# Attention scan in chunks of 64 tokens instead of 128, in a one-core audio tower kernel

## The reference

```python
def step(carry, inp):
    A, z = carry
    qt, kt, vt = inp
    A = lam[None, :, :, None] * A + kt[..., None] * vt[..., None, :]
    z = lam[None] * z + kt
    St = jnp.einsum('bhi,bhij->bhj', qt, A)
    Zt = jnp.einsum('bhi,bhi->bh', qt, z)
    return ((A, z), (St, Zt))
_, (S, Zs) = jax.lax.scan(step, (A0, z0), (qT, kT, vT))
...
att = (S / Zs[..., None]).reshape(Bx, Tx, Cx)
att = g * att @ Wo.T
x = x + att
h2 = layernorm(x, ln2_g, ln2_b)
x = x + jax.nn.gelu(h2 @ W1.T, approximate=False) @ W2.T
```

## Time and profile before

| | us |
|---|---|
| median of 3 runs | 1092.09 |
| span of the profiled execution | 1090.0 |
| TensorE (PE) busy | 1058.7 (97%) |
| VectorE (DVE) busy | 886.6 (81%) |
| ScalarE (ACT) busy | 702.5 (64%) |
| GpSimd (POOL) busy | 293.5 (27%) |

### The profile page before, as it was taken

The page is one execution under the profiler, slowest core; times in us unless marked ns, Lnnn a source line. Parts: engine busy times, 40 slices in busy tenths (PEclk is TensorE's granted clock), DMA queues, the critical chain, the costliest instruction groups (busy, mean ns, idle before and its releaser), DMA issues.

```text
span 1090.0 us, 44778 instructions
## 1 busy us (share of the span) xinstructions
PE 1058.7 (97%) x18851; PEld 800.2 (73%) x18851; DVE 886.6 (81%) x2749; ACT 702.5 (64%) x1258; POOL 293.5 (27%) x177
## 2 busy tenths in 40 slices
PE   6789999999999999999999999999999999999987
PEld 6668677877767778687877867777786777868664
DVE  6889788888988879788887988878788887979642
ACT  3357676576666757576575767657676675758643
POOL 5322132331223222132332223232122322213120
PEclk9799999999999999999999999999999999999999
DMA  5532133122312322132232312313242232214110
GB/s 179 168 91 88 52 94 102 60 89 72 125 51 74 106 76 89 51 127 70 65 97 73 108 51 78 117 59 89 60 130 57 74 105 77 71 51 127 52 39 18
DMA packets 51510, 91.55 MB, mean 84 GB/s; under 512 B 9552, under 2 KB 26608, under 8 KB 51312
## 3 DMA queue, kind: packets, MB, share of 16 engines
q1 hardware_dynamic: 51312, 88.69, 26.7%
HBM read 19.50 MB, written 9.78 MB: 27 GB/s over the span
## 4 chain that ended last, share of the span: by engine, by line
PE 95%; DVE 2%; ACT 1%; issue 1%; POOL 0%; DMA 0%; SPq 0%; DVEq 0%; ACTq 0%; POOLq 0%
PE bank L999 13%; PE bank L1004 11%; PE bank L1148 11%; PE bank L1170 10%; PE bank L1141 10%; PE bank L1176 10%; PE bank L1103 7%; PE bank L1078 4%; PE bank L1081 3%; PE bank L1121 3%; PE bank L1164 3%; PE bank L1086 3%; PE bank L1125 3%; PE bank L1041 3%; PE bank L1030 2%; PE bank L1056 1%
## 5 line engine op out<-in xcount | busy, mean ns | idle before, releaser
L1170 PE MATMUL bank<-xa,f1w 128*128 128x512 f32 (+1 forms) x256 | 120.5, 575 | 0.9 <-issue 0.9
L1148 PE MATMUL bank<-w,hid 128*128 128x128 f32 x1024 | 119.7, 275 | 1.5 <-ACT hid L565 1.5
L1141 PE MATMUL bank<-c,w 128*128 128x512 f32 (+1 forms) x256 | 119.2, 570 | 0.9 <-ACT c L559 0.9
L1148 PEld LDWEIGHTS bank<-w,hid 128*128 128x128 f32 x1024 | 116.9, 192 | 2.9 <-ACT hid L565 2.9
L539 ACT ACTIVATE px<-bank 128x512 f32<-128x512 f32 (+1 forms) x128 | 72.8, 568 | 63.5 <-PE bank L1086 55.2
L419 POOL TENSOR_TENSOR rr<-vv,nhalf 128x4 f32<-128x4 f32 x32 | 32.4, 1012 | 294.9 <-DVE vv L823 294.9
L565 ACT ACTIVATE hid<-bank 128x512 f32<-128x512 f32 (+1 forms) x128 | 70.2, 565 | 63.7 <-PE bank L1141 61.9
L1176 PE MATMUL bank<-hid,f2w 128*128 128x512 f32 (+1 forms) x256 | 107.5, 563 | 0.0
L1103 PE MATMUL bank<-qx,ki 128*32 128x16 f32 x7680 | 102.2, 193 | 1.5 <-DVE ki L866 1.5
L1103 PEld LDWEIGHTS bank<-qx,ki 128*32 128x32 f32 x7680 | 92.7, 110 | 13.7 <-issue 13.7
L804 DVE COPY_PREDICATED px<-mask,bank 128x512 f32<-128x512 uint32 (+1 forms) x128 | 88.5, 691 | 13.5 <-ACT px L539 13.5
(11 more groups left out here) (142 smaller groups left out, 2447.9 us busy)
## 6 DMA issues: line engine op xcount, KB each, us to landing
qx<-qq SPq DMA_DIRECT2D x256, 96.0 KB, 2.2
hs<-hs SPq DMA_DIRECT2D x32, 532.0 KB, 3.9
v<-v_f SPq DMA_DIRECT2D x16, 512.0 KB, 6.0
gz<-gate_f SPq DMA_DIRECT2D x16, 512.0 KB, 3.0
xT<-in_xT SPq DMA_DIRECT2D x16, 468.5 KB, 3.2
f1w<-in_fc1T SPq DMA_DIRECT2D x16, 256.0 KB, 3.2
f2w<-g_dram SPq DMA_DIRECT2D x16, 256.0 KB, 3.3
out<-t_sum SPq DMA_DIRECT2D x16, 256.0 KB, 2.5
```

Source lines behind the costliest of these rows:

```text
L1141: mm(dst[:, 0:width[g]], w1[:, P * j:P * j + P], c1[:, cols(g)], start=True, stop=True).then_inc(w1_ok, 1)
L1148: last = mm(dst[:, P * i:P * i + P], hid[:, j, P * m:P * m + P], w2[:, j, :], start=(j == 0), stop=(j == 3))
L1170: mm(dst[:, 0:width[g]], f1w[:, P * j:P * j + P], xa[:, cols(g)], start=True, stop=True).then_inc(f1_ok, 1)
```

## The change

The scan's chunk is 64 tokens. The level `kw[1]` falls away, with its products (line 1078), its copies of keys and queries, and a sixth of each `qx` transfer. Scores become compact: 64 queries wide instead of 128. Both kinds of scores of a tile, between and inside groups, share one bank, and two banks (5 and 6) take turns; `pairs_a` and `pairs_b` are one function `pairs`, whose end releases ScalarE's copy. The products inside groups have 64 keys as weights and 4 x 8 queries as columns: 16 a full tile. The scan has 14 states; `us`, `chain` and `states` work on twice as many, and `scan` does 64 columns at a time. For the states of the two halves of a tile, `v` becomes two tiles, each with the other half of its partitions zero, filled by two DMAs; `us` reads them too and so waits for the DMAs, and `hand_v` stands in SyncE's order ahead of `spread(b, 0)` of the same sample. In `scan`, tile 0 now waits for the states.

```diff
 SyncE
-                sp.dma_start(v[:, :, :], v_f[:, :, :]).then_inc(v_in, 16)
+                for o in (0, 1):
+                    rows = slice(BLK * o, BLK * o + BLK)
+                    sp.dma_start(v[o][rows, :, :], v_f[rows, :, :]).then_inc(v_in, 16)
...
-                    hand_h2(b); hand_v(b); spread(b, 1); hand_gate(b); spread(b, 2); spread(b, 3)
+                    hand_h2(b); spread(b, 1); hand_gate(b); spread(b, 2); spread(b, 3)
...
-                    hand_h1(b); spread(b, 0)
+                    hand_h1(b); hand_v(b); spread(b, 0)
 ScalarE, pxs
-                n = WIN * windows[c]
-                act.wait_ge(pa_ok, nth(b, TILES, c + 1))
+                n = BLK * blocks[c]
+                act.wait_ge(pr_ok, nth(b, TILES, c + 1))
 VectorE, qlev, between
-                for at, m, skip in ((Q8, EIGHT, 0), (Q32, 2 * WIN, WIN), (Q64, P, P // 2)):
+                for at, m, skip in ((Q8, EIGHT, 0), (Q32, 2 * WIN, WIN)):
...
-                klevels(b, g, parts + [(kw[:, 0, :], 2 * WIN, WIN, WIN), (kw[:, 1, :], P, P // 2, P // 2)], kon_ok)
+                klevels(b, g, parts + [(kw[:, :], 2 * WIN, WIN, WIN)], kon_ok)
 TensorE, us
-                pe.wait_ge(v_ok, nth(b, 2, 2))
-                for c in range(NST):
+                pe.wait_ge(v_in, nth(b, 32, 32))
+                for i in range(NST):
                     for hd in range(HEADS):
                         r = slice(HD * hd, HD * hd + HD)
-                        last = mm(dst[r, c:HD * NST:NST], kcT[:, c, r], v_f[:, c, r], start=True, stop=True)
+                        last = mm(dst[r, i:HD * NST:NST], kcT[:, i // 2, r], v[i % 2][:, i // 2, r], start=True, stop=True)
 TensorE, pairs
-                if c:
-                    pe.wait_ge(px_ok, nth(b, TILES, c))
+                if c >= 2:
+                    pe.wait_ge(px_ok, nth(b, TILES, c - 1))
                 else:
-                    before(pe, px_ok, b, TILES, TILES)
+                    before(pe, px_ok, b, TILES, TILES - 1 + c)
...
-                if n == NW:
-                    t0 = Q64 + P // 2 * o
-                    for w in (0, 1):
-                        r = slice(WIN * w, WIN * w + WIN)
-                        mm(O[r, :, P // 2:P], kw[:, 1, k0 + WIN * w:k0 + WIN * w + WIN], x[:, :, t0:t0 + P // 2], start=True, stop=True)
...
                 for j in range(EIGHT):
-                    for w in range(n):
-                        t0 = P * (c % 2) + WIN * w
-                        last = mm(D[WIN * w:WIN * w + WIN, :, WIN * w + j:WIN * w + WIN:EIGHT], ki[:, j, k0 + WIN * w:k0 + WIN * w + WIN],
-                                  x[:, :, t0 + j:t0 + WIN:EIGHT], start=True, stop=True)
-                last.then_inc(pb_ok, 1)
+                    for o in range(blocks[c]):
+                        r, s0, t0 = slice(BLK * o, BLK * o + BLK), k0 + BLK * o, q0 + BLK * o
+                        last = mm(D[r, :, j:BLK:EIGHT], ki[:, j, s0:s0 + BLK], x[:, :, t0 + j:t0 + BLK:EIGHT], start=True, stop=True)
+                last.then_inc(pr_ok, 1)
 TensorE, scan
+                opened = False
+                for o in range(blocks[c]):
+                    i, t = 2 * c + o, s0 + BLK * o
+                    if i:
+                        for hd in range(HEADS):
+                            r = slice(HD * hd, HD * hd + HD)
+                            mm(S[r, t:t + BLK], ab[:, i - 1, r], qc[:, BLK * i:BLK * i + BLK], start=not opened, stop=False, skip_group_check=True)
+                        opened = True
+                pe.wait_ge(px_ok, nth(b, TILES, c + 1))
+                for o in range(blocks[c]):
+                    t = s0 + BLK * o
                     for hd in range(HEADS):
                         r = slice(HD * hd, HD * hd + HD)
-                        mm(S[r, s0:s0 + n], ab[:, c - 1, r], qc[:, P * c:P * c + n], start=True, stop=False, skip_group_check=True)
...
+                        last = mm(S[r, t:t + BLK], v[o][:, c, r], px[c % 2][:, hd, :], start=False, stop=True, skip_group_check=True)
```

More of the change, by code:

```diff
@@ L65, in program @@
     windows = [min(4, WINS - 4 * c) for c in range(TILES)]
-    NST = TILES - 1
+    blocks = [-(-windows[c] // 2) for c in range(TILES)]
+    NBLK = sum(blocks)
+    NST = NBLK - 1
+    KT = TILES - 1
     ctx = ExitStack()
@@ L91, in program @@
         zeros = sb("zeros", P)
[L92 removed]
+        tick = sb("tick", 5)
         nhalf = sb("nhalf", 2 * TILES)
@@ L207, in program @@
         place = {name: (i, n) for i, users in enumerate(USES) for n, (name, _) in enumerate(users)}
-        spare = [bank[i] for i in range(8) if i not in [BETWEEN, DIAG] + [place[n][0] for n in ("dct0", "dct1", "nT0", "nT1")]]
+        spare = [bank[i] for i in range(8) if i not in [*PAIRS] + [place[n][0] for n in ("dct0", "dct1", "nT0", "nT1")]]
         EARLY = 5
@@ L665, in _ @@
             V.memset(dec[:, :, :], 0.0).then_inc(s_pw, 1)
-            V.memset(bank[DIAG][:, :], 0.0)
-            V.memset(bank[BETWEEN][:, :], 0.0)
+            for i in PAIRS:
+                V.memset(bank[i][:, :], 0.0)
+            for tile in px:
+                V.memset(tile[:, :, :], 0.0)
+            V.memset(v[0][BLK:P, :, :], 0.0)
+            V.memset(v[1][0:BLK, :, :], 0.0)
             for tile in (k, ga, gate_f, c1, xa):
@@ new lines, in pairs @@
+                    pe.wait_ge(kin_ok, nth(b, 2, c // 4 + 1))
+                for o in range(blocks[c]):
+                    r, t0 = slice(BLK * o, BLK * o + WIN), Q32 + q0 // 2 + WIN * o
+                    mm(O[r, :, WIN:BLK], kw[:, k0 + BLK * o:k0 + BLK * o + WIN], x[:, :, t0:t0 + WIN], start=True, stop=True)
+                for j in range(1, NE):
+                    for w in range(windows[c]):
+                        r, t, s0 = slice(WIN * w, WIN * w + WIN), WIN * (w % 2) + EIGHT * j, k0 + WIN * w
+                        t0 = Q8 + q0 + WIN * w + EIGHT * j
+                        mm(O[r, :, t:t + EIGHT], ko[:, j - 1, s0:s0 + WIN], x[:, :, t0:t0 + EIGHT], start=True, stop=True)
```

134 lines of the change are left out of this document (56 added, 78 removed).

## The result

| | before | after |
|---|---|---|
| median of 4 runs each, us | 1092.66 | 1171.43 |
| ratio, 95% interval | | 1.0717 (1.0677 to 1.0757) |
| span of the profiled execution, us | 1090.0 | 1168.4 |

The change makes the kernel 79 us slower. The direction was forecast, the size was not: 36 us were forecast, and 1171 lies above the range that ended at 1150. Four executions in this document took 1513 to 3488 us where all others took 1083 to 1175; they are left out of every time and ratio, and g1, whose profiled execution is one of them, has no profile to read.

What follows compares the result with a forecast made beforehand. TensorE was taken as the bound, busy all 64.74 us of a round. Terms +2.5 - 2.9 + 0.9 + 0.6 + 1.0 = +2.1 us a round, times 16, plus 2 at the start, gave 1128 us, 8-in-10 range 1068 to 1150.

Steps and rivals of the forecast that it cites:

- Part 1: Inside products: 16 steps of 57 ns at 64-wide weights, +0.30 us a full tile, +2.5 us a round.
- Part 3: Changes of weight width on TensorE: nine more a round at 0.10 us each, +0.9 us a round.
- Part 2: Products between halves: one level goes, -0.41 us in each of 7 tiles, -2.9 us a round.
- The line between 32 and 128 wide: Inside products: step interpolated from 33 ns at 32-wide and 107 ns at 128-wide weights, giving 57 ns at 64.
- Part 4: Twice the states: `us` +0.5 and `scan` +0.1 us a round, GpSimd's spreading of about 5.1 us hidden.
- Part 5: Values ahead of queries: TensorE waits before tile 0's first product, +1.0 us a round, plus 2 us once at the start.
- signs that the forecast named: Tile 3's inside group about 1.0 us, `us` about 0.95, round near 66.8, about a microsecond's wait before tile 0.
- two signs of being wrong: Tile 3's inside group at or under 0.6 us, or no wait before tile 0.
- the weights' width is not the price: Rival: 64-wide inside products step like 32-wide ones, 33 ns; most of it near 1078 us; chance 0.20.
- the two without late queries: Rivals with no query wait before tile 0: 1110 us (0.15), or 1095 us with no drain at width changes either (0.08).
- loads and columns in turn: Rival: inside products' columns don't stream beside the next weight load, 84 ns a step, 1181 us; chance 0.05.

Runs made afterwards that it cites:

- g1: e3 with the two value tiles in one, so the states take 28 products (56 records) instead of 56 (112): 1084.97 us, ratio 0.9921.
- g2: g1 with the states' products also moved ahead of the second half of the weights products, apart from tile 1: 1085.71 us, ratio 0.9925.
- g6: g2 with the 64-wide inside products of the changed kernel: 1135.77 us, ratio 1.04.
- e1: The changed kernel with the query transfers issued ahead of the value transfers again: 1151.25 us, ratio 1.0533.
- e4: The kernel before with only the inside products made wide (64 keys as weights, 4 x 8 queries as columns): 1155.66 us, ratio 1.0564.
- h3: e4 with queries read and results written in runs of 8 instead of every eighth place: ratio 1.0515.
- g4: The kernel before with inside products still 32 keys wide but 4 x 8 queries as columns instead of 4 x 4: 1138.25 us, ratio 1.0413.
- k1: g4 with queries read in runs of 8, results still written to every eighth column: ratio 1.0.
- e3: The changed kernel with queries first again and inside products 32 keys wide again: 1116.72 us, ratio 1.0208.
- g3: The kernel before with the states' products issued twice, 112 records instead of 56: 1109.57 us, ratio 1.0147.
- h2: e4 with results written in runs of 8, queries still read at every eighth place: ratio 1.0584.
- h1: e4 with queries read in runs of 8, results still written to every eighth column: ratio 1.0543.
- k2: g4 with queries read and results written in runs of 8: ratio 1.0012.

## Why the prediction was wrong

With the runs the 79 us fall into four parts, from the ratios: the rest of the change wins 8 us (g2 to before), the wide inside products cost 52 (g6 to g2), twice the records for the states 15, in stops and slow clock (e1 to g6), and the late queries 20 (after to e1). The first two hang together: g2 has about 1 us a round of waits for VectorE and ScalarE that the wide products cover. On the old kernel, which has no such waits, they cost 62 (e4).

Start-to-start sums over all records of one undisturbed round, in us, against the forecast terms:

| | before | after | measured | forecast |
|---|---|---|---|---|
| inside products | 5.46 | 8.83 | +3.37 | +2.6 (Part 1, one change of Part 3) |
| products between groups | 6.37 | 4.15 | -2.22 | -2.1 (Part 2, eight changes) |
| states | 0.50 | 0.98 | +0.48 | +0.5 |
| scan | 3.55 | 3.89 | +0.34 | +0.1 |
| wait ahead of tile 0 | 0 | 1.34 | +1.34 | +1.0 |
| the rest | | | +0.34 | 0 |
| round | 64.61 | 68.26 | +3.65 | +2.1 |

*Part 1* was the right mechanism with a size a little off. The line between 32 and 128 wide gave 57 ns; h3 has 58, and reading at every eighth place makes it 60. From its start to the next product the group takes 1.105 us, where the forecast had 1.02 with the change of width (0.92 and 0.10). Together that is +0.8 a round, 12 us. But the sentence that 16 against 32 columns matter little was right only for columns that lie side by side: its witness, `us`, reads runs of 32. g4 and k1 show this. That this did not change the sum is luck: both limits happen to give the same step.

*Part 2 and Part 3* hold. A change from 32 to 64 wide adds 0.11 us (0.126 against 0.02, e4 and g4), where 0.10 was taken. The pause agrees with the Trainium skill (TensorEngine Tiling (Array Packing), "Tiling Modes"), by which a change of tiling mode drains the engine; what happens in it no row shows.

*Part 4* holds for the time of the states (+0.48). `scan` was put too low: +0.34 a round, not +0.1. GpSimd's spreading stayed hidden but for 1.7 us in the first sample. The step that failed is in what was costed: "`us` has 112 records instead of 56 at 9 ns: +0.5" prices records at the rate at which TensorE works them off and asks nothing about how they get there. The runs show that such a row of small records is paid for a second time: TensorE has worked off its block of 256 instructions before the next has come, stands still in tile 1, and the clock is halved at times. That cost 15 us in the changed kernel (e1 to g6), 32 with narrow inside products (e3 to g1), and 8 beyond its own time in the old one (g3).

*Part 5* holds: a wait stands ahead of tile 0 in every round, 1.4 us by e1 against 1.0. Behind the values each query issue takes up to 0.74 us (2.96 for four) where 0.6 was assumed. At the start it is 3.2 us where 2 were added, and 2.9 in the last sample.

The miss is 43 us. Some 25 are from terms of the undisturbed round (1.55 times 16), 12 of them from the inside products. Stops and half-clock stretches in the middle rounds are some 12 (15.5 less the 3.6 that the kernel before has too). The start and the end hold some 8 more than the forecast 2: the first denominators are at 53.6 instead of 47.4 us, and from the last ones to the end it is 83.2 instead of 78.8. For these last two I have no experiment that parts them further, and they overlap with the first sum; the first denominators stand anywhere from 48.4 to 51.0 us in the runs that only alter the inside products of the old kernel, so part of the 6 us may be no more than that spread.

The signs that the forecast named mostly came true: the inside group of tile 3 at 1.11 us, `us` at 0.95, a wait ahead of tile 0, and neither of the two signs of being wrong; only the round was 68.2 us instead of 66.8. They are read in one good round, and so say nothing of what only happens in some.

The rivals: "the weights' width is not the price" is refuted by e4 and h3 as far as the time goes, and the two without late queries by the wait in every round; "loads and columns in turn" came out at 1181, near the 1171 measured, but by an 84 ns step that isn't there: the step is 60. A near number is no evidence for a mechanism. What stays open is why the clock falls in some rounds. In after a fall follows 3.4 us in which TensorE was busy for only 1.92, and in e3 falls follow stops of 2 us; but in g6 all three, and in after and e1 five of thirteen, come right behind a group of denominators with TensorE busy throughout, and the kernel before has one behind denominators too, at 754.9.

## What to carry to other kernels

Count instructions before adding up their times. Where hundreds of small matmuls stand in a row, fewer of them with more columns gain more than the record rate says: halving one such group took the ratio from 1.0208 to 0.9921 (e3 to g1). When an engine stands still with nothing to wait for, look at the queue that brings its instructions, and at the number of the instruction where it goes on.

Widen a matmul in its columns, read side by side, and not in its weights: 32 columns in runs cost nothing over 16, while 64-wide weights lengthen the step from 39 to 58 ns and add 0.11 to 0.15 us where the width changes. When a step is priced by another group, compare how that group reads its operands, not only how much. And read more than one round: the good one hid more than a quarter of this miss.

## What the runs showed of the hardware

- TensorE's instructions come in packets of 16,384 bytes, one for 256 instructions, on their own DMA queue. Where some 200 small records are worked off in 2 us the next block is late: TensorE stands still for up to 2.1 us, always at the same place of a block, until 1.2 to 1.6 us after the packet has landed (41 stops in fifteen traces).
- A product with 32-wide weights steps at 36 to 40 ns in its strip with 16 columns at every eighth place or 32 in runs of 8 (k1), and at 60 ns with 32 at every eighth place (g4).
- A product with 64-wide weights and 32 columns steps at 58 ns when they are read in runs (h3) and at 60 ns at every eighth place (e4). Other numbers of columns were not run.
- The stride of the results costs nothing (e4 to h2, h1 to h3, k1 to k2).
- A change of width: 0.126 us from record to record for 32 to 64, where it is 0.02 without a change; 0.12 for 32 to 128; 0.15 to 0.17 for 64 to 128 or to 32.
- Half the granted clock came in stretches of 3.4 us, at times two or three in a row, behind waits and stops, and in g6 behind the denominators alone.
